# A transformer with routed experts on one core: attention copies and products one to two slots later, four transposed buffers, the routing tail spread over two steps, two evacuations on VectorE, one root chain for two LayerNorms

## The reference

```python
h = clip(sum(|conv2x2(x)|), 0, 1); h = concat([h, table[x_txt]])        # 16 x 333 x 256
h = h + attention(layernorm(h))     # 16 heads of 16, windows of 128 tokens every 64, one more at the end,
                                    # softmax(q k / 4 + pos_bias) v, mean over the windows of a token, Wo
x = layernorm(h)                    # (x - mean) / sqrt(var + 1e-5)
scores = softmax(x @ gate_w.T)      # 8 experts, the best 2 for each token
h = h + sum over the 2 of score * (silu(x @ w1[e]) * (x @ w3[e])) @ w2[e]
```

## Time and profile before

| what | value |
|---|---|
| median of 3 runs | 1401.97 us (1401.92 to 1404.63) |
| the profiled execution, its time | 1394.69 us |
| its span, first to last instruction | 1392.9 us |
| busy share PE / DVE / ACT / POOL | 85% / 66% / 56% / 44% |
| attention stage with the start-up, to the first expert matmul | 872.3 us |
| expert stage | 520.6 us |

### The profile page before, as it was taken

The page is one execution under the profiler, slowest core; times in us unless marked ns, Lnnn a source line. Parts: engine busy times, 40 slices in busy tenths (PEclk is TensorE's granted clock), DMA queues, the critical chain, the costliest instruction groups (busy, mean ns, idle before and its releaser), DMA issues.

```text
span 1392.9 us, 35049 instructions
## 1 busy us (share of the span) xinstructions
PE 1189.1 (85%) x10190; PEld 951.8 (68%) x10191; DVE 920.9 (66%) x4211; ACT 782.9 (56%) x3176; POOL 611.8 (44%) x900
## 2 busy tenths in 40 slices
PE   2386888988988998888889872999999999999996
PEld 1254656655655665555556551999999999999995
DVE  4485989888888889898997864344444444444442
ACT  0196998989899998899899980211111111111110
POOL 5333466565646655665665334122322232232232
PEclk9698899889898988999998985899999999999998
DMA  3694563465357446634643507232233323323222
GB/s 110 133 234 100 109 132 89 95 131 113 88 103 142 92 92 116 128 89 94 133 107 71 96 24 234 36 50 46 49 47 48 49 45 49 48 46 48 46 49 31
DMA packets 98402, 123.36 MB, mean 89 GB/s; under 512 B 15544, under 2 KB 87416, under 8 KB 95192
## 3 DMA queue, kind: packets, MB, share of 16 engines
q1 hardware_dynamic: 75880, 89.96, 30.6%
q0 software_dynamic: 18576, 24.47, 10.9%
q10 hardware_dynamic: 3808, 7.34, 1.8%
HBM read 69.35 MB, written 46.07 MB: 83 GB/s over the span
## 4 chain that ended last, share of the span: by engine, by line
PE 47%; POOL 16%; issue 14%; DMA 12%; ACT 4%; SPq 3%; DVE 3%; POOLq 0%; DVEq 0%; ACTq 0%
PE s_bank L1168 12%; PE t_bank L1168 12%; PE o_bank L1183 11%; DMA qk_parts<-parts_flat 5%; POOL expert_slots L493 4%; DMA expert_slots<-rows,slot_i 4%; DMA stacks<-qk_parts 3%; PE m_bank L1104 3%; ACT probs L622 3%; PE t_bank L1040 2%; SPq L372 2%; POOL rest L502 2%; PE o_bank L1063 2%; POOL parts_flat L507 2%; PE m_bank L1157 1%
## 5 line engine op out<-in xcount | busy, mean ns | idle before, releaser
L622 ACT ACTIVATE probs<-probs,neg_max 128x128 f32<-128x128 f32 x1280 | 497.4, 401 | 21.6 <-DVE neg_max L757 21.0
L757 DVE CUSTOM_DVE_ANT_0 probs<-s_bank,nbias 128x128 f32<-128x128 f32 x1280 | 293.0, 284 | 38.4 <-PE s_bank L1026 36.9
L622 ACT ACTIVATION_READ_ACCUMULATOR probs<-probs,neg_max 128x1 f32 x1280 | 257.4, 201 | 0.0
L1040 PE MATMUL t_bank<-ident,probs 128*128 128x128 f32 x1280 | 221.0, 300 | 28.7 <-ACT probs L622 26.7
L681 ACT ACTIVATE v_all<-s_bank 128x512 f32<-128x512 f32 x91 | 54.4, 598 | 286.9 <-PE s_bank L1168 286.9
L1026 PE MATMUL s_bank<-stacks 96*128 96x128 bf16 x1280 | 136.5, 233 | 68.8 <-DMA stacks<-qk_parts 46.9
L1026 PEld LDWEIGHTS s_bank<-stacks 96*128 96x128 bf16 x1280 | 93.4, 105 | 132.4 <-DMA stacks<-qk_parts 50.7
L1040 PEld LDWEIGHTS t_bank<-ident,probs 128*128 128x128 f32 x1280 | 150.1, 153 | 45.7 <-ACT probs L622 41.7
L636 ACT ACTIVATE probsT<-t_bank 128x512 f32<-128x512 f32 x240 | 141.9, 591 | 57.5 <-PE t_bank L1040 56.7
L1183 PE MATMUL o_bank<-stacks,v_all 128*128 x728 | 172.6, 380 | 0.7 <-issue 0.5
L597 POOL DMA_INDIRECT out_dram<-wq_sb,nbias x46 | 75.7, 1645 | 198.5 <-DVE wq_sb L967 185.3
(11 more groups left out here) (158 smaller groups left out, 2079.4 us busy)
## 6 DMA issues: line engine op xcount, KB each, us to landing
stacks<-qk_parts SPq DMA_DIRECT2D x192, 166.5 KB, 5.6
qk_parts<-parts_flat SPq DMA_DIRECT2D x192, 83.2 KB
nbias<-expert_slots SPq DMA_DIRECT2D x91, 129.0 KB, 2.0
w_sb<-in_L_ffn_w_dram ACTq DMA_DIRECT2D x14, 512.0 KB, 5.2
v_all<-v_all SPq DMA_DIRECT2D x64, 96.0 KB, 6.4
x_here<-in_x_dram SPq DMA_DIRECT2D x16, 256.0 KB, 5.7
out_dram<-h_res SPq DMA_DIRECT2D x16, 256.0 KB
stacks<-in_L_ffn_w_dram SPq DMA_DIRECT2D x8, 512.0 KB, 8.5
```

Source lines behind the costliest of these rows:

```text
L622: ins = act.activation(seg, seg, ACT.Exp, bias=neg_max[:, r, i:i + 1], scale=-1.0, accum_out=row_sum[:, (par + v) % 2, h:h + 1])
L757: ins = dve.tensor_tensor_reduce(probs[:, r, i * WIN:(i + 1) * WIN], s_bank[:, k % 2, i * WIN:(i + 1) * WIN], nbias[:, h, :], 1.0, BIG, AL ...
L1040: mm = pe.transpose(t_bank[:, (k - 3) % 2, i * WIN:(i + 1) * WIN], probs[:, r, i * WIN:(i + 1) * WIN], ident[:, :])
```

## The change

Per engine, by slot (before, then now):

- **PE**: products with v (L1063) for group k-4, now k-6. v projection in slots 10 and 11, now 6 and 7; output projection in 6 and 7, now 10 and 11. Logits in slot 18 of the step, now in slot 3 of the next one; counts in slot 2, now 8. `x2T` transposes in slot 16, now 18.
- **ACT**: the copy to `probsT` stands at the head of slot k+3, where it stood at the end of slot k+2; its order against the exponentials stays. The copies of `xT` and `x2T` out of PSUM are gone from ACT.
- **DVE**: has these two copies (`xT` in slot 1, `x2T` in slot 19). Its copy to `probsT` and the spread move from slot 5 to slot 7 (mod 4). `part_high` from 4 and 6 to 5 and 7, `part_middle` from 6 and 8 to 8 and 10. v's bias from 12 and 14 to 8 and 9. Best two from 19 to slot 4 of the next step; the rest of the routing from 0, 2 and 3 to 6, 10 and 9. LN1's moments from 15 to 5. The sum and the clip of the image are gone from DVE.
- **POOL**: has the sum and the clip (slot 3). The six scatters move from slots 4 to 9, between the splits, to 11 to 13, behind them. One root chain for both LayerNorms on tiles twice as wide, in slot 14, where two stood in 11 and 16.
- **SP**: the shifts of v stand ahead of the load of the k stack, and the store of `h_res` behind it. `w3` of expert 6, whose space now holds two of the four `probsT` buffers, is loaded at the end of the attention stage.

```diff
-        probsT = sb("probsT", [P, 2, GH * WIN])
+        probsT2 = sb("probsT", [P, 2, GH * WIN])
+        probsT = [probsT2[:, i, :] for i in range(2)] + [w3_sb[:, E - 2, c, :] for c in range(C)]
...
                     load_stack(0, q_stack[par1], Q_SLOTS)
                     write_part(1, 2, part3_ready)
-                    if tail:
-                        store_h2()
-                    load_stack(1, k_stack[par1], K_SLOTS)
                     vt = v_win[par1]
...
+                    load_stack(1, k_stack[par1], K_SLOTS)
+                    if tail:
+                        store_h2()
...
+            sp.wait_ge(pv_done, B * G)
+            sp.dma_start(w3_sb[:, E - 2], w3[E - 2].rearrange("(c p) n -> p c n", p=P)).then_inc(expert_weights_in, 16)
...
+                    if inp and k == 3:
+                        pool.wait_ge(conv_step, b2 * 3 + 2)
+                        pool.tensor_tensor(diag[:, :, :], diag[:, :, :], anti[:, :, :], ALU.add).then_inc(conv_step, 1)
...
-                    if proj and k == 5:
+                    if proj and k == 6:
                         split_rest(0)
...
+                    if tail2 and k == 11:
                         pool.wait_ge(slots_ready, b9 + 1)
                         pool.wait_ge(payload_ready, b9 * 4 + 4)
...
+                    if (inp or tail) and k == 14:
...
+                        if tail:
+                            pool.wait_ge(ln2_step, b0 * 6 + 6)
+                        inverse_roots(b2)
...
+                    if proj and k == 1:
+                        dve.wait_ge(xT_done, b1 + 1)
...
+                        dve.tensor_copy(xT[:, :, :], m_bank[:, :, 0:S]).then_inc(xT_ready, 1)
...
-                    if proj and k == 8:
+                    if proj and k == 10:
                         part_middle(1)
...
+                    if proj and k == 8:
                         if b1 >= 2:
                             dve.wait_ge(pv_done, (b1 - 1) * G)
+                        part_middle(0)
                         add_v(0, 0)
                         add_v(1, 2)
...
-                    if (k >= 4 and att) or (k < 4 and tail):
+                    if (k >= 6 and att) or (k < 6 and tail):
...
-                    if tail and k == 18:
-                        pe.wait_ge(x2T_ready, b0 + 1)
+                    if tail2 and k == 3:
+                        pe.wait_ge(x2T_ready, b9 + 1)
```

More of the change, by code:

```diff
@@ L785, in step @@
                             .then_inc(head_ready, 1)
-                    if tail2 and k == 0:
+                    if tail2 and k == 4:
+                        dve.wait_ge(logits_done, b9 + 1)
+                        dve.tensor_copy(logits[:, :, :], o_bank[:, par, 0:NT * E].rearrange("p (j e) -> p j e", j=NT))\
+                            .then_inc(logits_read, 1)
+                        dve.wait_ge(logits_read, b9 + 1)
+                        for j in range(NT):
+                            dve.max(best[:, j, :], logits[:, j, :]).then_inc(best_ready, 1)
+                        for j in range(NT):
+                            dve.wait_ge(best_ready, b9 * 6 + 1 + j)
+                            dve.max_index(best_i[:, j, :], best[:, j, :], logits[:, j, :]).then_inc(best_ready, 1)
+                    if tail2 and k == 6:
                         if b9 >= 1:
@@ L806, in step @@
                             .then_inc(taken_ready, 1)
-                    if tail2 and k == 2:
+                    if tail2 and k == 10:
                         dve.wait_ge(score_e_ready, b9 + 1)
```

326 lines of the change are left out of this document (151 added, 175 removed).

## The result

The changed kernel takes 1451.23 us (median of four runs, 1451.07 to 1458.03) against 1401.95: 1.0358 of the time before, interval [1.0326, 1.0391], so 49.3 us slower. The forecast was 1442 in a range of 1385 to 1480, with 0.70 on slower.

The account below looks back on a forecast made before the run. The loop over the stacks was taken as the bound: k middle part's end plus transfers. 13 steps x 2.8 = +36 us and +4 at the end gave 1394.7 + 40 = 1435, or 1442 on the median, range 1385 to 1480.

Parts of the forecast that it names:

- What bounds the kernel: Attention stage: a loop from first scores to the next stacks; DVE's end of the k middle part, then transfers, set it.
- First stretch: PE, slots 0 to 5: logits add 1.2 us, LN1's normalisation wait saves 1.0; slot 6's scores end at +15.9.
- VectorE up to the k middle part: DVE, slots 6 to 10: 11.6 us of instructions back to back; k middle part ends at +27.5, was +25.2.
- The held copy: DVE's spread in slot 7, which a POOL split can hold: taken as unheld, otherwise 1.6 us more in a step.
- Transfers: From the k middle part's end to the next scores: 21.5 us plus 0.5 for scatters beside the q stack, 22.0.
- A step: Each of 13 attention steps with routing: 27.5 + 22.0 = 49.5 us against 46.75, +2.8.
- five signs: Steps 49 to 50 us; stack wait over 2; middle part 27 to 28; about 22 after; LN1 roots wait gone.
- The end: Drain: batch 14's logits before the last products, routing work before the scatters; 4 us taken of 2.4 + 3.0 - 0.6.
- The total: Whole kernel: +40 us, 1394.7 + 40 = 1435, or 1442 on the runs' median.
- A: Attention steps: the slots, not the stacks, set the step, about 45 us at ACT's pace; 1363 us, chance 0.25.
- B: Slots 0 and 1 lose up to 3 us at 2.4 GHz, loop unchanged; 1400 to 1412 us, chance 0.20.
- C: Attention steps: held spread (1.6) and scatters in the way (2.1), 6.0 us longer; 1484, counted from 1460; chance 0.15.

## Why the prediction was right, by its steps

**What bounds the kernel** was right: the loop over the stacks, divided at the k middle part. The places' move and the move to slot 11 shift the step by about as much as they shift that part, and the rest stays within 22.2 to 23.5 us in the eight kernels where most steps begin with a wait for the stack (the one whose q stack is held back on purpose apart). What the prediction did not see is how near the next limit stands: 1.7 us shorter and the slots, with the late completions in them, take over.

**First stretch**: +15.9 for slot 6, measured +15.89. Its parts (1.2 from the clock, 1.0 from the roots' wait) were chosen between wide bounds and not measured one by one, so that agreement to 0.01 is luck. The base was one step, too, the shortest of the 13 before (46.75 against a mean of 48.00); by the means the scores of slot 6 came 0.5 us earlier (+15.58 against +16.07), not 0.2 later.

**VectorE up to the k middle part**: 11.6 was foretold, 12.55 measured. The list of what stands in front was complete from slot 6 on; what is over is one held instruction.

**The held copy** is the step that failed by its place. I named the spread in slot 7 and took it as free; it is free, 0.28. But the places' product now begins 0.07 us behind the split of k, ends with it, and was held for 1.2 us. The Trainium skill, "SBUF — State Buffer", section "SBUF: two separate sides", names VectorE's operations with two SBUF inputs, as this product is, among those that the lock can hold beside a GpSimd operation that reads SBUF; the trace agrees. With a hold looked for at every instruction ahead of the middle part instead of at the spread alone, the sum would have been +28.7 (27.5 + 1.2); the mean is 28.55, and with the places moved it is 26.92.

**Transfers**: +0.5 was taken, +0.7 came, but not by the mechanism named. SP's order, costed at nothing, saves 0.66; about 1.3 is lost to something else. Bytes of the scatters in the way was my reason, the standstill is another; no run of the changed kernel tells them apart or shows that the scatters are behind it.

**A step**: +2.8 foretold, +3.42 measured. Of the five signs two were missed, by the held product and the transfers: the steps are 51.42 and not 49 to 50, the middle part ends at +28.55 and not at 27 to 28. **The first two steps**: nothing foretold, 2.2 measured. **The end**: +4 foretold, +9.7 measured. 3.4 of it lie in the last step with attention (from its first scores to its last it takes 41.65 us instead of 38.29), where the scatters of batch 13 run from 855.70 to 863.13 and ScalarE's and VectorE's waits of 2.5 and 3.1 us for "remote" end at 864.6 and 864.4: the standstill again, with no stack to hide it. The drain has the other 6.3. From the last scores to the last roots it took 19.2 us (824.33 to 843.50) and takes 22.4 (874.36 to 896.73), +3.2, about what I had priced. But from there to the logits of batch 15 it is 9.4 instead of 7.2: the normalisation waits for the landing of batch 14's scatters (L901), which were issued by 896.66, and starts at 902.74, 2.1 us after the roots are out. And from those logits to the scatters it is 7.2 instead of 6.2, because the weights of batch 15 now stand behind the places and the scatters wait for them. I had named the landing for a middle step and not looked for it in the last.

**The total.** Against its own profiled time the sum was 1435 and came out at 1451. The 7.3 us that I added for the median of before had no counterpart after. So the median came within 9 us by 16 us of undersized terms, and 7 that fell away.

**The rivals.** A (the slots set the step) is wrong for both kernels as they are, and right as soon as the loop is shortened. Its own point, 4.0 us earlier, was met by the two kernels with the short loop that were made from before (middle part at +21.25 and +19.76), and its gain did not come. B's sign was right in the first slots (0.40 for the first scores instead of 0.61, the upper clock level), but slot 6 came only 0.5 us earlier, with the logits now in front of it. C named a hold and the scatters as the two prices: a hold of 1.2 came, at another instruction, and no run shows the bytes. Two of its figures don't follow from the sums: half of C's 82 us gives 1443, not 1460, and B's +24.5 to +25.5 gives 1403 to 1416 with the 22.0 of transfers, not 1400 to 1412.

**Left open**: why the steps stay at 48 us when no stack is waited for. The engines' busy time in such a step is at most 43.2 of 47.8 us (ScalarE), some 2.6 us are the row of four scatters, and the rest is handed from engine to engine; no single wait in the list stands for it. A kernel with the short loop in which no two scatters follow each other was not tried. Open, too, is what the standstill needs besides a row of scatters, since the profile of before has rows of three without it.

## What to carry to other kernels

Look for the loop that closes over a transfer, divide it where one engine hands over, and cost an edit by how far it moves that point; then look at what stands behind the loop, for the gain ends there. Check every instruction of VectorE ahead of the point, small ones too, against what GpSimd does at that time in its new place. Do not put indirect scatters in a row while other engines wait for TensorE: spread them between other work (six in one row cost 60 us here; a kernel with none in a row was not measured).

## What the runs showed of the hardware that was not expected

While GpSimd issues scatters one behind another (about 1.0 us each, 1.3 apart), TensorE's completions can reach the other engines late and then in a burst. By the times of the semaphore updates the first one held is of a matmul that ends 1 to 2.5 us after the first scatter begins, and the burst is over 0.4 to 2 us after the last. The longest delay grows with the row: two, 1 to 1.7 us; three, about 2 (three behind the splits) to 3 (k middle part in slot 10, before); four, about 3; six, 6 to 7 (6.7 in the row shown). But in the profile of before rows of three in 13 steps, and one of four, leave no delay at all, with the same transfers beside them, so there is another condition, which isn't known. GpSimd's own chain runs on. It happens with and without the stack's transfers, so these are not needed; whether it is the issuing or the scatters' own packets, and what in the chip holds the completions back, no run shows. The row of six cost 60 us of 1402 in the kernel before, the largest effect of any single move here. The list of waits shows it as waits on ScalarE and VectorE for "remote" where it is long, and under TensorE's own name where it is short, beside a TensorE that has nothing left to do.
